# A two-layer attention kernel on one core: another order of row groups and banks, the exponent table loaded elsewhere, and the first layer's value projections copied out of PSUM by VectorE instead of ScalarE

## The reference, cut to what matters

```python
q = split_heads(layernorm(x) @ Wq.T + bq)          # 16 heads x 128 x 16
k = split_heads(ctx @ Wk.T + bk)                   # 16 heads x 12544 x 16
v = split_heads(ctx @ Wv.T + bv)
scores = einsum('bhqd,bhkd->bhqk', q / sqrt(16), k)
scores = scores + ((1.0 - attention_mask) * -10000.0)[:, None, :, :]   # first attention only
probs = softmax(scores, axis=-1)
ctx_out = einsum('bhqk,bhkd->bhqd', probs, v)
```

## Time and profile before

| what | value |
| --- | --- |
| median of 3 runs | 979.61 us (978.74 to 981.27) |
| profiled execution, its own time | 976.58 us |
| span of the profiled execution | 974.9 us |
| PE, VectorE, ScalarE, GpSimd busy | 928.5, 701.2, 701.1, 398.6 us |
| mean granted clock of TensorE | 0.996 of full |

### The profile page before, as it was taken

One profiled execution on the slowest core, in us unless ns is written; L12 is line 12 of the kernel. 1 busy time (PEld: TensorE's weight loads), 2 busy tenths in 40 slices (PEclk: granted clock), 3 DMA queues, 4 the chain that ended last, 5 costly groups with the idle time before them and its releaser, 6 DMA issues.

```text
span 974.9 us, 37261 instructions
## 1 busy us (share of the span) xinstructions
PE 928.5 (95%) x16290; PEld 575.1 (59%) x16291; DVE 701.2 (72%) x1531; ACT 701.1 (72%) x1003; POOL 398.6 (41%) x365
## 2 busy tenths in 40 slices
PE   8899999999999999998887799999999999999987
PEld 3355666666666666655653456666666666666666
DVE  5788888888888988966348766566656656666566
ACT  2778998998898899887554556666666666666752
POOL 4268888778888878884100100112102010110000
PEclk9999999999999999999999999999999999999999
DMA  9512201211221110123023001011101101000000
GB/s 341 157 40 68 89 24 67 89 27 66 87 82 32 68 56 8 68 94 134 1 72 146 2 2 45 5 44 46 45 3 46 46 4 44 13 3 3 3 2 6
DMA packets 14995, 53.09 MB, mean 54 GB/s; under 512 B 4336, under 2 KB 5744, under 8 KB 10992
## 3 DMA queue, kind: packets, MB, share of 16 engines
q1 hardware_dynamic: 14832, 50.70, 15.2%
HBM read 50.56 MB, written 0.13 MB: 52 GB/s over the span
## 4 chain that ended last, share of the span: by engine, by line
PE 53%; issue 32%; DVE 7%; ACT 4%; POOL 3%; DMA 1%; SPq 0%; DVEq 0%; POOLq 0%; ACTq 0%
PE ps_out L1503 11%; PE ps_scores L1482 9%; PE ps_proj L1406 9%; PE ps_proj L1421 8%; PE ps_max L1428 5%; PE ps_scores L1478 2%; POOL k_high L580 2%; DVE tile_max L1040 1%; ACT probs L766 1%; PE ps_scores L1421 1%; DVE probs L1109 1%; POOL tern L628 1%; DMA bq<-in_L_xattn_bq 1%; ACT probs L760 1%; DVE unread L1037 1%
## 5 line engine op out<-in xcount | busy, mean ns | idle before, releaser
L1040 DVE TENSOR_REDUCE tile_max<-ps_max 128x1 f32<-128x512 f32 (+1 forms) x293 | 188.3, 674 | 137.5 <-PE ps_max L1428 135.3
L589 POOL TENSOR_TENSOR probs<-probs,masks 128x512 f32<-128x512 f32 x180 | 227.3, 1284 | 78.0 <-ACT probs L752 78.0
L766 ACT ACTIVATE probs<-ps_scores 128x1024 f32<-128x1024 f32 x192 | 186.3, 1021 | 71.4 <-PE ps_scores L1482 70.8
L760 ACT ACTIVATE probs<-probs 128x1024 f32<-128x1024 f32 x196 | 206.7, 1055 | 42.9 <-DVE probs L1098 32.1
L1482 PE MATMUL ps_scores<-q_pad,k_full 32*128 32x256 f32 x3072 | 234.5, 375 | 0.0
L1037 DVE CUSTOM_DVE_ANT_0 unread<-ps_max,masks 128x512 bf16<-128x512 f32 (+1 forms) x294 | 190.5, 675 | 49.3 <-PE ps_max L1428 48.8
L1503 PE MATMUL ps_out<-probs,values 128*32 128x128 f32 x6272 | 217.3, 277 | 1.6 <-DVE ps_out L1081 0.4
L1503 PEld LDWEIGHTS ps_out<-probs,values 128*32 128x32 f32 x6272 | 159.2, 110 | 56.3 <-issue 48.9
L1482 PEld LDWEIGHTS ps_scores<-q_pad,k_full 32*128 32x128 f32 x3072 | 187.2, 185 | 8.2
L1428 PE MATMUL ps_max<-k_high,q_high 32*128 32x512 bf16 (+1 forms) x591 | 155.8, 381 | 15.3 <-DVE tile_max L1040 8.8
L1406 PE MATMUL ps_proj<-wv,ctx_t 128*32 128x256 f32 x2752 | 165.2, 380 | 0.1
(11 more groups left out here) (302 smaller groups left out, 865.6 us busy)
## 6 DMA issues: line engine op xcount, KB each, us to landing
ctx_t<-in_ctx_t SPq DMA_DIRECT2D x23, 1024.0 KB, 5.9
masks<-in_mask_n SPq DMA_DIRECT2D x12, 512.0 KB, 3.7
masks<-in_mask_t SPq DMA_DIRECT2D x12, 512.0 KB, 3.9
room_w<-in_L_attn_f_w SPq DMA_DIRECT2D x2, 1024.0 KB, 7.9
room_w<-in_L_ffn_w SPq DMA_DIRECT2D x2, 1024.0 KB, 7.7
ctx_t<-in_ctx_t SPq DMA_DIRECT2D x2, 512.0 KB, 6.0
room_w<-in_L_ffn_w_gate SPq DMA_DIRECT2D x1, 1024.0 KB, 11.0
room_w<-in_L_ffn_w_up SPq DMA_DIRECT2D x1, 1024.0 KB, 13.5
```

The source lines that it names most:

```text
L589: nc.gpsimd.tensor_tensor(p, p, three(mask_t[m % 2], GT)[:, t, :].unsqueeze(1).to_broadcast([P, 4, P]), ALU.add).then_inc(sig("bias_added" ...
L760: nc.scalar.activation(prob(T, half), prob(T, half), ACT.Exp).then_inc(sig(f"exp_done{half}"), 1)
L766: nc.scalar.activation(prob(T, half), scores_in(m, t, half).rearrange("p a n -> p (a n)"), ACT.Exp).then_inc(sig(f"exp_done{half}"), 1)
L1040: ins = v.tensor_reduce(tile_max[:, h, 1 + half:2 + half], max_bank(m, j)[:, 0:width(m)], AX_X, ALU.max)
```

## The change

- In `scores` the four row groups are issued in the order 2, 3, 0, 1, or 0, 1, 2, 3 where the maxima just ahead were in groups 2 and 3. The two halves of a tile's scores now have a signal each, and those who wait for the scores wait for their half; in layer 1 the exponent of the half that was issued first comes first.
- An exponent of one column is put on ScalarE in two places: behind the copies of the queries in layer 0, and between `max_out` and `rows_out` in layer 1. The third `abs_sum` moves from the first tile to a place before the first maximum.
- The bank of a maximum is the one that was used longest ago. In tiles of layer 1 that have no projection and aren't lone (all of block 13, and tile (24, 0)) there are three to choose from. The counts and one chain of blocks 13 and 14 change: block 13 makes 50 maxima in place of 46, block 14 makes 36 in place of 40.
- In layer 0 `values_out` moves from ScalarE to VectorE, behind the maximum chain and ahead of the maxima `ahead`, for every tile that isn't lone: 45 copies of 128x512.

```diff
@@ -218,7 +218,7 @@
-        CHAINS = {(NG, SPLIT - 2): NG + 1, (NG, 5): NG + 2, (NG + 1, 0): NG + 3}
+        CHAINS = {(NG, SPLIT - 2): NG + 1, (NG, 5): NG + 2, (NG, 7): NG + 3}
@@ -285,20 +285,39 @@
                 own = ((2, 2, 2), (2, 2, 2), (2, 2, 0))[t] if t < SPLIT - 1 else own
-                now = ((0, 0, 0), (0, 0, 0), (0, 0, 2), (2, 2, 2), (2, 2, 2), (2, 0, 2), (2, 2, 2), (2, 2, 2))[t]
+                now = ((0, 0, 0), (0, 0, 0), (0, 0, 4), (2, 2, 2), (2, 2, 2), (2, 2, 2), (2, 2, 2), (2, 2, 0))[t]
             elif m == NG + 1:
-                own = (2, 0, 0) if t == 0 else own
-                now = ((0, 0, 2), (2, 0, 2), (2, 2, 2), (2, 2, 2), (2, 2, 2), (2, 0, 2), (2, 2, 0), (0, 0, 0))[t]
+                now = (2, 2, 2) if t in (2, 4) else (2, 0, 2) if t < chain_at(m) else (2, 0, 0) if t == chain_at(m) else now
             elif m == 0:
...
                 now = (2, 0, 2 if t < chain_at(m) else 0)
-            if n + 2 < NG and m != NG:
+            if m == NG:
+                ahead = (0, 0, 2) if t == size(m) - 1 else ahead
+            elif n + 2 < NG:
                 ahead = (0, 0, 2) if t == chain_at(m) else (2, 0, 2) if t > chain_at(m) else ahead
...
+        KEYS_AT = {0: 0, 2: 1, 4: 2, 6: 3}
+        VALUES_AT = {1: 0, 3: 1, 5: 2, 7: 3}
+        def keys_at(m, t):
+            k = m + 2
+            if t in KEYS_AT and k < BLOCKS and k not in (NG + 1, NG + 2) and KEYS_AT[t] < key_units(k):
+                return k, KEYS_AT[t]
+            return None
+        def values_at(m, t):
+            k = m + 1
+            if t in VALUES_AT and k < BLOCKS and k not in (NG, NG + 1) and VALUES_AT[t] < value_units(k):
+                return k, VALUES_AT[t]
+            return None
+        def three_banks(m, t):
+            return m >= NG and not keys_at(m, t) and not values_at(m, t) and not lone(m, t)
@@ -313,11 +332,20 @@
             read = {bank: maxima0(NG * l) + (2 * H, H)[l] for bank in range(2)}
-            turn_of, turned_here = 0, {}
+            order, turned_here = [0, 1, 2], {}
+            def take(bank):
+                order.remove(bank)
+                order.append(bank)
+                return bank
+            def oldest(count):
+                return take([bank for bank in order if bank < count][0])
             if l == 0:
...
                 for j in range(FIRST_AHEAD):
-                    MAX_BANK[1, j], MAX_AFTER[1, j], BEHIND_TURN[1, j] = j, read[j], None
+                    MAX_BANK[1, j], MAX_AFTER[1, j], BEHIND_TURN[1, j] = take(j), read[j], None
                     read[j] = maxima0(1) + j + 1
@@ -325,9 +353,9 @@
                         if k == 1 and turns_in(m, t) and not lone(m, t):
-                            TURN_BANK[m, t], TURN_AFTER[m, t] = turn_of, read[turn_of]
-                            turned_here[turn_of] = turns_in(m, t)
-                            turn_of = 1 - turn_of
+                            bank = oldest(2)
+                            TURN_BANK[m, t], TURN_AFTER[m, t] = bank, read[bank]
+                            turned_here[bank] = turns_in(m, t)
                         here = []
@@ -335,22 +363,22 @@
                                 done[to] = upto
-                        swapped = k == 0 and len(here) == 2 and (m == 0 or m >= NG) and sum(count[1] for count in counts) == 2
-                        two = k == 0 and len(here) == 2 and not swapped
+                        visits = sum(count[1] for count in counts) == 2
                         for i, (to, j) in enumerate(here):
-                            if i == 0 and two or i == 1 and swapped:
-                                MAX_BANK[to, j] = 2
+                            if three_banks(m, t):
+                                bank = oldest(3)
+                            elif k == 0 and len(here) == 2 and i == int(visits):
+                                bank = take(2)
                             else:
-                                MAX_BANK[to, j], MAX_AFTER[to, j] = turn_of, read[turn_of]
-                                BEHIND_TURN[to, j] = turned_here.pop(turn_of, None)
-                                read[turn_of] = maxima0(to) + j + 1
-                                turn_of = 1 - turn_of
+                                bank = oldest(2)
+                            MAX_BANK[to, j] = bank
+                            if bank < 2:
+                                MAX_AFTER[to, j] = read[bank]
+                                BEHIND_TURN[to, j] = turned_here.pop(bank, None)
+                                read[bank] = maxima0(to) + j + 1
                         MAXIMA[m, t].append(here)
...
@@ -420,6 +436,15 @@
         TAPS_AT = NG + 3
+        def row_groups(m, t):
+            k, s = (m, t - 1) if t else (m - 1, size(m - 1) - 1)
+            used = [max_of(*x)[3] for x in MAXIMA[k, s][2]] if (m, t) not in ((0, 0), (NG, 0)) else []
+            return [0, 1, 2, 3] if 2 in used or 3 in used else [2, 3, 0, 1]
+        def first_half(m, t):
+            return row_groups(m, t)[0] // 2
@@ -695,7 +720,8 @@
                 if j == 0 and m > 2:
-                    act.wait_ge(sig("scores_ready"), 2 * tile0(m - 2))
+                    for half in range(2):
+                        act.wait_ge(sig(f"scores_ready{half}"), tile0(m - 2))
                     act.wait_ge(sig("k_high"), 2 * (m - 2) - 1)
@@ -737,7 +763,8 @@
                 if m > 1:
-                    act.wait_ge(sig("scores_ready"), 2 * tiles_to(m - 2))
+                    for half in range(2):
+                        act.wait_ge(sig(f"scores_ready{half}"), tiles_to(m - 2))
                     act.wait_ge(sig("max_changes"), decays(m - 1))
@@ -746,7 +773,7 @@
             def copy_second(T):
-                act.wait_ge(sig("scores_ready"), 2 * T + 2)
+                act.wait_ge(sig("scores_ready1"), T + 1)
                 need("pv_done", T - 1)
@@ -761,7 +788,7 @@
                 T = tile0(m) + t
-                act.wait_ge(sig("scores_ready"), 2 * T + half + 1)
+                act.wait_ge(sig(f"scores_ready{half}"), T + 1)
                 need("pv_done", T - 1)
@@ -785,7 +812,7 @@
                     keys_out(*keys_at(m, t))
-                if values_at(m, t):
+                if values_at(m, t) and (m >= NG or lone(m, t)):
                     values_out(*values_at(m, t))
@@ -805,6 +832,8 @@
                 nc.scalar.copy(q_pad[:, :, :].rearrange("p c n -> p (c n)"), ps_max[:, 1, :]).then_inc(sig("q_copied"), 1)
+                if l == 0:
+                    nc.scalar.activation(stat[:, 40:41], ones[:, 0:1], ACT.Exp).then_inc(sig("exp_loaded"), 1)
                 if l == 1:
@@ -818,9 +847,11 @@
                         first_out(u)
-                        if u in (7, 8):
+                        if u in (7, 8, 9):
                             abs_sum(u - 7)
                 max_out(NG * l)
+                if l == 1:
+                    nc.scalar.activation(stat[:, 41:42], ones[:, 0:1], ACT.Exp).then_inc(sig("exp_loaded"), 1)
                 rows_out(NG * l)
@@ -837,8 +868,6 @@
                             copy_second(T)
-                            if T == 0:
-                                abs_sum(2)
                             decays_out(m, t)
@@ -849,8 +878,8 @@
                             decays_out(m, t)
-                            exp_scores(m, t, int(lone(m, t)))
-                            exp_scores(m, t, 1 - int(lone(m, t)))
+                            exp_scores(m, t, first_half(m, t))
+                            exp_scores(m, t, 1 - first_half(m, t))
                             lent_out(m, t)
@@ -1075,6 +1104,14 @@
+            def values_out(m, u):
+                dve.wait_ge(sig("v_ready"), values0(m) + u + 1)
+                at = tiles_of(u)
+                if m > 1:
+                    dve.wait_ge(sig("pv_done"), tile0(m - 2) + min(at.stop, size(m - 2)))
+                v.tensor_copy(values[m % 2][:, at, :, 0:HD],
+                              ps_proj[:, 0:D * (at.stop - at.start)].rearrange("p (t h d) -> p t h d", h=H, d=HD)).then_inc(sig("v_copied"), 1)
             def decay_sums(s):
@@ -1093,7 +1130,7 @@
                     dve.wait_ge(sig("bias_t"), 2 * m + 1 + (t > 0))
-                dve.wait_ge(sig("scores_ready"), 2 * T + 1)
+                dve.wait_ge(sig("scores_ready0"), T + 1)
                 need("pv_done", T - 1)
@@ -1105,7 +1142,7 @@
                 for half in (1, 0):
-                    dve.wait_ge(sig("scores_ready"), 2 * T + 1 + half)
+                    dve.wait_ge(sig(f"scores_ready{half}"), T + 1)
                     v.tensor_tensor(prob(T, half).rearrange("p (h q) -> p h q", h=8),
@@ -1185,6 +1222,8 @@
                             chain(chained(m, t))
+                        if l == 0 and values_at(m, t) and not lone(m, t):
+                            values_out(*values_at(m, t))
                         for k, j in ahead:
@@ -1473,16 +1512,17 @@
                 banks = [scores_in(m, t, g // 2)[:, g % 2, :] for g in range(4)]
```

(7 more changed lines are left out.)

12 lines of the change are left out of this document (removed).

## The result

The changed kernel takes 982.93 us (median of 13 runs, 980.46 to 988.61); the kernel before takes 978.61 us beside it (13 runs). The ratio is 1.0046, 95% interval 1.0031 to 1.0062: slower by more than the 0.3% that this kernel can tell. The forecast was 985.3 us and slower.

A forecast was written before the change was run, and what follows sets the result against it. TensorE (PE) was taken to bound layer 0's steady tiles. The terms +11.6 + 0 - 1.9 + 1.0 - 5.0 = +5.7 took the profiled 976.58 to 982.3; the median's extra 3.0 gave 985.3 us, range 977 to 991.

The forecast's parts named there:

- my own case: Whole kernel: the terms hold as summed, a time between 982 and 989 us, chance 58%.
- late table: Start of layer 1: table load and small exponent delay the row copy and PE's first scores, +1.0 us, bounds 0 and 1.5.
- Value copies: Layer 0 tiles with value copies on VectorE: first ahead read 0.31 us late, tile as much longer; +11.6 us in all.
- Rival (a): Layer 0: the copies stay in VectorE's 0.60 us of idle time, kernel faster at 973.7 us; 10%.
- Rival (b): Layer 0: the copy is short, 0.42 us, costing +4.8 us; 978.5 us, no change; 15%.
- Rival (d): All of layer 0: VectorE becomes the bound, each copy costs 0.61 us, 27 in all; 1001 us; 4%.
- Row groups: Scores of nearly every tile: each row group waits for itself alone, so the new order is worth 0.
- rival (e): Scores in some 170 tiles: the row order returns 0.21 us each, 36 us in all; 949 us; 3%.
- Early table: First tiles of layer 0: exponent table load and third sum moved earlier, -1.9 us, bounds 0 and -3.2.
- Three banks and counts: Blocks 13 and 14: a third bank and new counts of maxima, -5.0 us, bounds -1.5 and -8.5.
- Rival (c): Block 13: three banks bring nothing since chain and row turn set it; 990.3 us; 10%.

The follow-up runs named there:

- half copy: The changed kernel with VectorE copying only the first of each pair of value tiles from block 2 on, half the values left out: 972.5 us.
- copy between the reads: The changed kernel with VectorE's value copy behind the first of the two ahead reads instead of before both: 997.53 us.
- the values back: The changed kernel with the value copies of layer 0 back on ScalarE: 973.08 us.
- double: The changed kernel with VectorE making each value copy twice, the second behind a wait for the first: 1012.19 us.
- delay: The changed kernel with three ScalarE passes of 512 columns in place of layer 1's one-column exponent, the table loaded behind the row copy: 982.28 us.
- exponent behind the queries: The changed kernel with value copies on ScalarE and layer 1's one-column exponent moved behind the copies of the queries: 967.95 us.

## Why the prediction came out right, point by point

**Direction and size.** Slower with 71%, 985.3 us for 982.9; inside the range and inside my own case. The sum said +5.7, the runs +4.3, and the other 1.0 us between forecast and time is the kernel before, which took 978.61 in the longer series and 979.61 in the first. Two terms held nearly as written, the values were 1.6 too high, and two others, rows and late table, were mis-sized with opposite signs. That the total came within 1.4 us is in part luck.

**Value copies: right.** Forecast +11.6 from 0.61 between starts and 0.31 of delay a tile. Both numbers stand in the trace of after; t = 5 takes 4.81 for 4.64, 0.17 where I had 0.1. Blocks 1 to 9 are 1.07 longer each, forecast 1.03. The whole is 9.9 us by taking the part away, 10.0 by adding it alone (11.1 by the medians), and 10.1 in the blocks of the traces. The difference to 11.6 is at the ends of the layer. In block 0 the tiles behind t = 1 and t = 3 grew by 0.09 each and not by 0.31, and the extra 0.3 for tile 1 did not come. In block 10 they grew by 0.31, but its tile 7 became 0.4 shorter, and tile 5 of block 11 0.35. The forecast had nothing that could become shorter; what ScalarE gave up may have been worth something there, but I did not trace it. Rival (a), hidden copies, fell. Rival (b), a short copy, fell too, though the half copy shows that its reasoning holds: with 0.34 from copy to read, the read is 0.06 late (200.29 - 199.81 for 200.13 - 199.71) and the tile 0.03 longer. Rival (d), VectorE as the bound, fell: the tiles without a value projection kept their 4.27. With the copy between the reads blocks 1 to 9 take 36.9 us, 1.3 more, without VectorE having more to do. The order on VectorE sets the cost, not its load.

**Row groups: the 36 us of rival (e) did not come, but 0 was too little.** In the steady tiles the new order is worth nothing, as the earlier trace rows said; rival (e) would have given 3.6%, and 0.21% was measured. The strict program order of the Trainium skill (TensorE: Matmul & The Clock Gate, Part 3, The mechanism) is not what these traces show. The step that failed in this term is "separate signals for the halves let ScalarE start a copy up to 0.2 earlier, off the path". At layer 1's end the exponent is on the path. There order and signals together gave 0.2 to 0.3 us in a tile with half a unit of projection and some 0.1 in one with none, 1.4 us in blocks 23 and 24; the whole was 2.1 by the ratio and 1.1 by the medians. Order and signals were not taken apart.

**Early table: right.** Forecast -1.9, tile 1 of block 0 gave -1.5 in each kernel that has it, the block -1.6, the ratio -2.6 (interval -4.1 to -1.3). One thing may lie between these: two of the four profiled executions without it (only the values, only the banks) have 3.4 us at half clock in block 0, and tile 1 takes 8.5 us there, not 6.9. With it, one of ten has such a stretch (tile 2 takes 8.0 for 6.4 with the delay).

**Late table: the step that failed.** "+1.0, bounds 0 and 1.5." The term priced the delay alone. The delay was 0.9; the cost was 4.5 and 4.1 us, in the two pairs with and without the exponent. In the changed kernel the engine falls to 1.2 GHz for 6.8 us at layer 1's start, and the tiles (13, 0) and (13, 1) take 4.95 and 4.79 us where they take 3.62 and 3.70 without it: 2.4 us. Over the profiled executions: where first scores are late (the change, the values back, copy between, half, double, delay) six of six have half clock from within 0.8 us of the first scores of layer 1, for 6.8 or 10.2 us. Where they aren't (before, the four single parts, no late exponent with and without the values, exponent behind the queries) two of eight do. PE's wait in front of these scores in the changed kernel, where the earlier trace rows have 0.74:

```profile
532.82 0.40 PE L1518 MATMUL ps_scores<-max_rows,minus 32*128 32x512 bf16 x4 [1.63 <-issue]
```

The delay without the table shows that it is the delay that costs 4 us. That the half clock is how it costs them is the reading that fits, and 0.9 plus 2.4 is still 1 us short of 4.1 to 4.5. The profiled executions are one run a kernel, and the change's had less half clock than its others: where a stretch of 10.2 us was followed by one of 3.4 in the same block (four of the six) block 13 took a further 2.6 to 2.9 us.

The mean granted clock on record for every run closes most of that gap. Time at half clock is twice the span times what the clock lacks to 1. The 13 runs of the change have a mean clock of 0.9942, 11.5 us at half clock; the 11 without the late exponent have 0.9986, 2.7 us. A straight line through both kernels' spans gives 0.38 us for each microsecond at half clock, and 1.0 us (standard error 0.5) for the exponent at an equal clock: (11.5 - 2.7) x 0.38 + 1.0 = 4.3 of the 4.5, as an estimate. The pair with the values back gives 0.45 and 1.0 (0.2), with 13.6 and 8.7 us at half clock: 3.2 of the 4.1. So the forecast of 1.0 was the right price of the delay, and what it left out was the clock. Half clock is likelier with the late scores, not certain: one of the change's 13 runs had a mean clock of 1.000, and of the 40 runs of the six kernels with late scores it is the only one at 0.999 or more. Of the 21 runs of the three kernels with the same banks, row order and early table and with the scores on time, 11 are.

**Three banks and counts: right.** Forecast -5.0; alone it gave 0.9950, -4.9. Block 13 at the full clock takes 32.6 (forecast 33.6), block 14 36.3 (36 to 37.5). Rival (c) fell. With the row order alone the profiled execution had both blocks at the full clock without the banks, 35.4 and 37.7 us: so 2.8 and 1.4 of the gain are not the clock's. The forecast's share for the clock is not shown. No profiled execution with the banks has half clock in block 14, but of the four without them only two have, and over its runs the kernel with the banks alone has the same mean clock (0.9943) as the kernel before (0.9939).

**The sum as measured.** +10.0 for the values, -2.1 rows, -4.9 banks, -2.6 early table, +4.3 late table (the mean of 4.5 and 4.1): +4.7, and +4.3 was measured. The parts' intervals reach 1.2 to 1.9 us to either side, so this agreement is closer than they can promise. The late table was 3.3 too low in my sum, the rows 2.1 and the values 1.6 too high: that these have opposite signs is why the total is so near, and that is luck.

## What to carry to other kernels

When a copy is moved to another engine because that one has idle time, look at which buffers the copy and its new neighbours release, and who waits for both: two releases that ran side by side on two engines come one behind the other on one. With the copy first the cost in a tile is the time from its start to the next pass's start, less the idle time that it can use (here 0.61 less 0.30, 0.31 us); with the copy second it was more, 0.59 us in the tiles behind t = 1 and t = 3. A load of the exponent table is worth moving only into a stretch where its engine waits anyway; the same load gained 1.5 us (together with the moved `abs_sum`), cost 4 or cost nothing by its place. Price a delay at a place where TensorE already waits with the clock in mind, and check it with an experiment that has the delay alone.

## What the runs showed of the hardware

- Two passes of 0.69 us on VectorE started 0.61 us apart where no wait for the first stood between them, and 0.72 apart in the double copy, where the second waited for the first one's signal.
- The load of the exponent table took 1.28 us each time, and an exponent that waited for nothing else began 0.01 us behind it.
- TensorE's clock fell to 1.2 GHz for 3.4, 6.8 or 10.2 us at a time in these profiled executions, at the start of layer 0, in block 10 and in blocks 13 and 14. Around layer 1's first scores it did so in six profiled executions of six where PE had waited 1.6 to 1.7 us in front of them, and in two of eight where it had waited 0.74. In the 9 us before, PE had further waits of 0.74 for VectorE and 0.98 for ScalarE in both cases.
- Mean granted clock over all runs of a kernel: 0.9939 before (29 runs), 0.9938 to 0.9943 with one of the four parts alone, 0.9986 with all four and no late exponent (11 runs), 0.9942 with the late exponent (13 runs). No part alone raised it; together they did.
- In block 13, where PE and VectorE take turns, 6.8 us at half clock cost 2.4 us, not the 3.4 that half of them would be (an estimate for a PE that is never idle).
- Row groups and banks are two separate conditions. With the old order too, scores started in free groups while others were blocked: three at 526.85 and the fourth 0.10 later. All four were held, for 0.23 us at 883.14, where the banks of the free groups were busy as well.
